# Rounding the normalised features and taking their remainder before the transposition instead of after it, in a four-layer graph network kernel

## What is computed

```python
h = jnp.maximum(_layernorm(x, axis=-1), 0.0); x = x + _L0_gnn_ref(h, adj, ...)   # Chebyshev, K = 4
h = jnp.maximum(_layernorm(x, axis=-1), 0.0); x = x + _L1_gnn_ref(h, adj, ...)   # encoder, 2 attentions, MLP
h = jnp.maximum(_layernorm(x, axis=-1), 0.0); x = x + _L2_gnn_ref(h, adj, ...)   # graph convolution
h = jnp.maximum(_layernorm(x, axis=-1), 0.0); x = x + _L3_gnn_ref(h, adj)        # sum over neighbours
```

## Time and profile before

| | |
|---|---|
| median of 3 runs | 913.66 us |
| the profiled execution: its own time | 909.79 us |
| its span, first to last instruction | 908.0 us |
| TensorE busy | 775.2 us, 85% |
| VectorE busy | 593.0 us, 65% |
| ScalarE busy | 447.5 us, 49% |
| GpSimd busy | 406.3 us, 45% |
| mean granted TensorE clock | 0.973 of full speed |

### The profile page before, as it was taken

One profiled execution on the slowest core, in us unless ns is written; L12 is line 12 of the kernel. 1 busy time (PEld: TensorE's weight loads), 2 busy tenths in 40 slices (PEclk: granted clock), 3 DMA queues, 4 the chain that ended last, 5 costly groups with the idle time before them and its releaser, 6 DMA issues. The chain is left out here.

```text
span 908.0 us, 13130 instructions
## 1 busy us (share of the span) xinstructions
PE 775.2 (85%) x3808; PEld 542.7 (60%) x3808; DVE 593.0 (65%) x1631; ACT 447.5 (49%) x929; POOL 406.3 (45%) x491
## 2 busy tenths in 40 slices
PE   3658798989999798989979898997989899898874
PEld 2435566666667566666756666664666666675543
DVE  3265677686776668677666767766776867765432
ACT  2044646547273644737364463736465472744430
POOL 3144545445553434555443455544454455533301
PEclk9869999999999999999999999999999999999996
DMA  5000101001020200101010010102010010000000
GB/s 170 32 1 1 52 1 40 20 1 59 1 59 0 60 0 6 53 0 58 0 59 0 12 46 0 58 0 59 0 49 9 0 58 0 6 2 6 1 6 6
DMA packets 29264, 22.54 MB, mean 25 GB/s; under 512 B 19488, under 2 KB 21024, under 8 KB 29216
## 3 DMA queue, kind: packets, MB, share of 16 engines
q1 hardware_dynamic: 29216, 22.03, 8.3%
HBM read 19.93 MB, written 2.10 MB: 24 GB/s over the span
## 5 line engine op out<-in xcount | busy, mean ns | idle before, releaser
L605 ACT ACTIVATE negz<-negz,negmax 128x512 f32<-128x512 f32 x128 | 92.3, 721 | 96.8 <-DVE negmax L821 95.7
L425 POOL TENSOR_TENSOR rstd_post<-vareps_post,nhalf 128x4 f32<-128x4 f32 x32 | 39.1, 1221 | 196.2 <-DVE vareps_post L708 196.2
L821 DVE CUSTOM_DVE_ANT_0 negz<-negz,gate 128x512 f32<-128x512 f32 x128 | 102.7, 802 | 23.8 <-DVE negz L815 23.6
L1075 PE MATMUL turn_ps<-pt,v_n 128*128 128x512 f32 x256 | 117.4, 602 | 0.0
L425 POOL TENSOR_TENSOR rstd_pre<-vareps_pre,nhalf 128x4 f32<-128x4 f32 x32 | 34.1, 1067 | 149.5 <-DVE vareps_pre L708 149.5
L955 PE MATMUL pre_ps<-at_hi,u_pair_pre 128*128 128x512 f32 x192 | 87.4, 455 | 7.4 <-DVE u_pair_pre L745 5.2
L815 DVE TENSOR_TENSOR negz<-score_ps,a_nat 128x512 f32<-128x512 f32 x128 | 88.0, 687 | 7.6 <-PE score_ps L1044 5.3
L955 PE MATMUL post_ps<-at_hi,u_pair_post 128*128 128x512 f32 x128 | 55.8, 436 | 38.4 <-DVE u_pair_post L745 38.4
L564 ACT ACTIVATE y_t_pre<-pre_ps 128x512 f32<-128x512 f32 x48 | 28.7, 597 | 118.4 <-PE pre_ps L955 117.6
L1058 PEld LDWEIGHTS turn_ps<-ident,negz 128*128 128x128 f32 x512 | 60.9, 141 | 33.7 <-ACT negz L605 14.6
L955 PE MATMUL pre_ps<-at_lo,u_pair_pre 128*128 128x512 f32 x192 | 78.5, 409 | 0.0
(11 more groups left out here) (138 smaller groups left out, 1838.3 us busy)
## 6 DMA issues: line engine op xcount, KB each, us to landing
a_nat<-in_adj SPq DMA_DIRECT2D x16, 1024.0 KB, 5.7
x_in<-in_x SPq DMA_DIRECT2D x16, 128.0 KB, 2.3
out<-x_out SPq DMA_DIRECT2D x16, 128.0 KB, 1.9
cheb_ws<-in_L_gnn_weight SPq DMA_DIRECT2D x2, 64.0 KB, 5.0
att_w<-in_L_gnn_a_wv SPq DMA_DIRECT2D x2, 64.0 KB, 2.7
att_w<-in_L_gnn_a_wk SPq DMA_DIRECT2D x2, 64.0 KB, 2.5
att_w<-in_L_gnn_a_wq SPq DMA_DIRECT2D x2, 64.0 KB, 2.3
bv_f<-in_L_gnn_a_bv SPq DMA_DIRECT2D x2, 64.0 KB, 2.8
```

The lines of the kernel that those rows point to most:

```text
L425: gp.tensor_tensor(rstd[t][:], vareps[t][:], nhalf[:, 0:RB], ALU.pow)\
L605: sc.activation(probs[:, i, :], negz[:, i, :], ACT.Exp, bias=negmax[:, i:i + 1], scale=-1.0, accum_out=total[:, i:i + 1]).then_inc(probs_d ...
L821: ve.tensor_tensor_reduce(negz[:, i, :], negz[:, i, :], gate[:, i, :], -1.0, 3.0e38, ALU.add, ALU.min, negmax[:, i:i + 1]).then_inc(biased, 1)
L1075: mm = te.matmul(turn_ps[0][:], v_n[a][:, j * P:(j + 1) * P], pt[:, j, :], start=(j == 0), stop=(j == RB - 1))
```

## The change

Both norms now write plain features (`h_nat`, 64 numbers a node) and then a new pair tile `h_pair` of type `float32r`: the rounded features first, and beside them the remainder, a subtraction over 128 x 256 elements. TensorE transposes the pair. ScalarE's copy then yields both parts at once. The step `split_ht` is gone from VectorE, both steps `cheb_ht` and `enc_ht` from its order, and TensorE waits for ScalarE's copy. `set_bias_rows`, which runs once, moves from the first `enc_ht` to the first `norm_enc`.

```diff
@@ vector order
-        split_at2-0 split_at3-0 attend.2-2 mask0.1-1 mask1.1-1 cheb_ht-0 mask2.1-1 
+        split_at2-0 split_at3-0 attend.2-2 mask0.1-1 mask1.1-1 mask2.1-1 
-        mask0.2-1 cheb_fold1-0 stats_enc-0 norm_last-2 mask1.2-1 norm_enc-0 mask2.2-1 enc_ht-0  mask3.2-1  last_fold-2""".split(),
+        mask0.2-1 cheb_fold1-0 stats_enc-0 norm_last-2 mask1.2-1 norm_enc-0 mask2.2-1  mask3.2-1  last_fold-2""".split(),
@@ tiles
-        h_nat = {"pre": sb("h_nat_pre", [P, RB, 2, C]), "post": sb("h_nat_post", [P, RB, C])}
+        h_nat = {t: sb(f"h_nat_{t}", [P, RB, C]) for t in ("pre", "post")}
+        h_pair = sb("h_pair", [P, RB, 2, C], F32R)
@@ def norm_apply(t, chain, g, k):
-                to = h_nat[t][:, :, 0, :] if t == "pre" else h_nat[t][:]
-                one = ve.scalar_tensor_tensor(to, centred[t][:], 0.0, over_blocks(rstd[t][:]),
+                one = ve.scalar_tensor_tensor(h_nat[t][:], centred[t][:], 0.0, over_blocks(rstd[t][:]),
                                               ALU.max, ALU.mult)
@@
                 chain.add(one)
                 dve.wait_ge(chain.sem, chain.so_far())
-                ve.tensor_copy(h_nat[t][:, :, 1, :], to).then_inc(h_ready[t], 1)
+                chain.add(ve.tensor_copy(h_pair[:, :, 0, :], h_nat[t][:]))
+                dve.wait_ge(chain.sem, chain.so_far())
+                ve.tensor_tensor(h_pair[:, :, 1, :], h_nat[t][:], h_pair[:, :, 0, :].bitcast(F32),
+                                 ALU.subtract).then_inc(h_ready[t], 1)
+                if first(g) and k == 1:
+                    set_bias_rows()
@@
-            def split_ht(g, k):
-
-                dve.wait_ge(ht_copied, 2 * g.n + k + 1)
-                ve.tensor_tensor(h_t[C:P, :], pre_ps[C:P, 0, :], h_t[C:P, :].bitcast(F32),
-                                 ALU.subtract).then_inc(ht_split, 1)
-                if first(g) and k == 1:
-                    set_bias_rows()
@@ def turn_h(ready):
                     mm = te.transpose(pre_ps[:, 0, i * P:(i + 1) * P],
-                                      h_nat["pre"][:, i, :, :].rearrange("p a c -> p (a c)"), ident[:])
+                                      h_pair[:, i, :, :].rearrange("p a c -> p (a c)").bitcast(F32),
+                                      ident[:])
@@ cheb_weights and encode on TensorE
-                pe.wait_ge(ht_split, 2 * g.n + 1)
+                pe.wait_ge(ht_copied, 2 * g.n + 1)
-                pe.wait_ge(ht_split, 2 * g.n + 2)
+                pe.wait_ge(ht_copied, 2 * g.n + 2)
```

More of the change, by code:

```diff
@@ L256, in graph_layers @@
         at_split = sem("at_split")
-        ht_split = sem("ht_split")
         u_split = {t: sem(f"u_split_{t}") for t in ("pre", "post")}
@@ L269, in graph_layers @@
         out_done = sem("out_done")
-        dve_pre = Chain(sem("dve_pre"), 2 * 6 + 6)
+        dve_pre = Chain(sem("dve_pre"), 2 * 7 + 6)
         dve_post = Chain(sem("dve_post"), 2 * 5 + 3 + 2)
@@ L466, in cheb_u3 @@
                 pool.wait_ge(dinv_done, g.n + 1)
-                pool_pre.add(gp.tensor_tensor(u3[:], h_nat["pre"][:, :, 0, :],
+                pool_pre.add(gp.tensor_tensor(u3[:], h_nat["pre"][:],
                                               over_blocks(dinv[g.slot][:, 0:RB]), ALU.mult))
@@ L886, in _ @@
                 "split_at1": split_at(1), "split_at2": split_at(2), "split_at3": split_at(3),
-                "cheb_ht": lambda g: split_ht(g, 0),
                 "cheb_weights": cheb_weights, "cheb_fold3": cheb_fold3,
@@ L890, in _ @@
                 "stats_enc": stats_enc, "norm_enc": enc_norm,
-                "enc_ht": lambda g: split_ht(g, 1),
                 **layer(0, mask0=mask(0), mask1=mask(1), mask2=mask(2),
```

## The result

The changed kernel takes 931.17 us (median of 4 runs, 929.95 to 932.27) against 913.39 us before (4 runs, 912.48 to 913.68). The ratio is 1.0196, with a 95% interval from 1.0177 to 1.0215: slower by 17.8 us, where 11.4 us were forecast. The profiled execution has a span of 930.4 us, 22.4 us more than the profiled one of before, at a mean granted clock of 0.956 instead of 0.973.

The account below looks back on a forecast made before the run. TensorE, busy 85% of the span, was taken to bound the kernel; 19.4 − 6.0 − 2.0 − 2.0 + 2.0 = +11.4 us on the 913.7 us median gave 925.1 us, range 915 to 938 us.

Parts of the forecast that it names:

- The holding of the subtraction: norm_cheb on VectorE: new subtraction held behind GpSimd's k_lo, delaying turn_a2 by 1.41 us a round; +19.4 us in all.
- slips in ahead of k_lo: Rival at norm_cheb: subtraction issues before GpSimd's k_lo, delaying turn_a2 only 0.46 us; −3.6 us, 910 us; chance 0.12.
- The two gains: On TensorE, cheb_weights starts 0.24 or 0.69 us sooner a round (−6.0 us), encode 0.13 us sooner (−2.0 us).
- The delay is taken up later in the round: Rival: TensorE waits that don't hang on turn_a2 absorb the delay; −10 us, 904 us; chance 0.05.
- The clock: Behind turn_a2 in the three rounds beginning a loop turn, longer waits lower the clock; +2 us (bounds 0 and +5).
- a rival: Clock falls behind turn_a2 in ordinary rounds too: eight give +12 us, 938 us, all eleven 942 us; chance 0.13.
- The first rounds: Graphs 0 and 1: set_bias_rows begins earlier, graph 1's norm precedes k_lo, two gaps close; −2.0 us (bounds −1 and −2.5).
- nothing behind `split_at` becomes late: ScalarE's copies, the row sum and GpSimd's inverse_roots move as much as TensorE, so cause no further delay; no size added.
- The reference point: Timed runs lie 3.9 us above the profiled execution of before; added to 921.2 us under the profiler, giving 925.1 us.

Follow-up runs that it names:

- e2: Kernel before plus a bn_stats over 128x256 (one SBUF input, result unused) behind the copy in norm_cheb: 920.25 us, ratio 1.0076.
- e4: Changed kernel with norm_cheb moved on VectorE from ahead of split_at0 to behind split_at3: 889.72 us, ratio 0.9747 to the kernel before.
- e3: Kernel before with the change for the encoder's features alone, the Chebyshev features still split behind their transposition: 905.89 us, ratio 0.9931.
- e6: Changed kernel plus seven matmuls with unread results ahead of turn_a2 on TensorE, from graph 2 on: 921.99 us, ratio 1.0107 to the kernel before.
- e8: The changed kernel run again unaltered, on the same chip as e5 and e6: 930.53 us, ratio 1.0190 to the kernel before.
- e5: Kernel before, without the change, with norm_cheb moved behind split_at3 on VectorE: 893.91 us, ratio 0.9771.
- e1: Kernel before plus a subtraction of two SBUF tiles (128x256, result unused) behind the copy in norm_cheb: 951.24 us, ratio 1.0411.

## Why the prediction was right, and where its size was off

**The holding of the subtraction (+1.41 us a round): right.** In the rounds of graphs 3 to 15 the trace after has 1.37 us for it and 1.70 us of wait at `turn_a2`, as written beforehand, and 4.04 us in the rounds that begin a loop turn. (In the round of graph 2, for which 1.1 us were booked, the subtraction was not held in this profile and the wait stayed at 0.20 us.) e2 shows that the holding makes it, and e4 that it costs nothing where nobody waits. The rival "slips in ahead of k_lo" fell: in every round from graph 3 on k_lo took over in the 0.03 us between the rounding's end and the subtraction's issue.

**The two gains (0.24 or 0.69, and 0.13 us a round): right.** TensorE's `encode` marks the rounds. In the round of graph 5, in which the clock stays up in both kernels, first before and then after:

```profile
252.81 0.50 PE L992 MATMUL pre_ps<-h_t,enc_hi 128*128 128x512 f32 x1 [0.36 <-DVE h_t L737]
303.54 0.50 PE L992 MATMUL pre_ps<-h_t,enc_hi 128*128 128x512 f32 x1 [0.36 <-DVE h_t L737]
```
```profile
259.28 0.47 PE L987 MATMUL pre_ps<-h_t,enc_hi 128*128 128x512 f32 x1
311.03 0.48 PE L987 MATMUL pre_ps<-h_t,enc_hi 128*128 128x512 f32 x1
```

That is 50.73 us before and 51.75 us after, +1.02 us, where the terms give 1.41 − 0.24 − 0.13 = +1.04 us. In the round of graph 8, of the other kind, it is 51.19 and 51.78 us, +0.59 us, where they give 1.41 − 0.69 − 0.13 = +0.59 us. "The delay is taken up later in the round" fell with this.

One thing in it was booked in the wrong place: 3.0 us of what was summed at `cheb_weights` are gained by the encoder's half alone (e3).

**The clock (+2 us): a mis-sized term.** In the profiled executions the rounds of graphs 3 to 15 grew by 18.2 us. The waits at `turn_a2` alone make 13 x 1.40 = 18.2 us; `cheb_weights` and `encode` give 5.5 and 1.8 us back; and so 18.2 − 18.2 + 5.5 + 1.8 = 7.3 us are left, which are the clock's: in five rounds `attend.2` to `cheb_ht` took 5.5 to 6.2 us instead of 4.13 us, and in four of the five `turn_a2` was slower too (1.60 to 1.97 us instead of 1.25 us). Before there are two such rounds. I had counted on the three rounds that begin a loop turn alone and given the ordinary ones to a rival. One ordinary round and the last one, with waits of 1.79 and 1.95 us, had it as well; so the rival was right in kind, and its eight or eleven rounds were too many. e6 bounds the term from above: filling takes back 8.5 us, about half of the 16.7 us by which e8 is slower than the kernel before on the same chip, but the two rounds of before are in it. The profile of e8 has the lower clock in the same five rounds as the profile of after.

**The first rounds (−2 us): wrong.** By `encode` of graph 2 the changed kernel was 2.75 us behind, where the terms of graphs 0 to 2 make it some 1.8 us ahead. I had let graph 1's norm move ahead of k_lo. In this profile it didn't:

```profile
63.26 1.38 DVE L724 TENSOR_TENSOR h_pair<-h_nat_pre,h_pair 128x256 fp32r<-128x256 f32 x1
```
```profile
65.38 1.22 PE L911 MATMUL pre_ps<-ident,a_nat 128*128 128x128 f32 x8 [1.58 <-DVE at_lo L733]
```

In the profile of e8, the same kernel, it did: k_lo had to wait for the keys until 62.61, and `turn_a2` waited for nothing.

```profile
62.46 0.42 DVE L724 TENSOR_TENSOR h_pair<-h_nat_pre,h_pair 128x256 fp32r<-128x256 f32 x1
```

TensorE's clock rose later in that execution (0.65 granted from 60 to 66 us, against 1.00 in the profile of after), which may be why the keys were late. And yet e8's `encode` of graph 2 came at 153.01 us, still 1.8 us behind the 151.22 us of before. So the order at k_lo is not what made the term wrong. In graph 0 I had said that nothing behind `split_at` becomes late. It did: with no other work on TensorE, `cheb_prop3` waits for GpSimd's `cheb_u3` (2.20 us before, 2.94 us after), and that hangs on ScalarE's row sums behind the third and fourth part. I had looked at the steady rounds only. Part of this is no effect of the change: the first adjacency matrix landed 0.37 us later in that execution.

**The reference point.** The forecast added the 3.9 us between the profiled execution and the timed median to both kernels. The timed executions of before in the job of e5 to e8 have spans from 909.7 to 913.0 us at clocks from 0.964 to 0.972; the profiled one had 908.0 us at 0.973. So the profiled one was a short execution, and what it lacked may have been drops of the clock, or time in the first rounds. For the second speaks e3: its rounds of graphs 3 to 15 are 6.5 us shorter than those of before in the profiles, just as its median is, but its `encode` of graph 2 came 4.1 us later (155.35 us), and so its profile shows a gain of 2.4 us only. No run separates the two.

**How near the number came by luck.** In the profiles the change costs 22.4 us, 11.0 us more than forecast: about 4.6 us of it up to `encode` of graph 2, 4.9 us in the rounds of graphs 3 to 15 (the clock's), and 1.5 us behind the last `encode`, which I haven't explained. The medians differ by only 17.8 us. The difference comes mostly from the reference: the profiled execution of before was 3.6 us shorter than its median, that of after 1.1 us longer. No term foresaw this, and it brought the number nearer to the forecast.

What stays open: why the clock fell behind a wait of 1.79 us in the round of graph 4 (1.78 us in e8, where it fell as well) and not behind the same wait in the rounds of graphs 7, 10 and 13. The runs show that filling the wait stops it, not which waits bring it about.

## What to carry to other kernels

Before an instruction of VectorE with two SBUF inputs, or a copy between SBUF tiles, is put into an order written by hand, lay GpSimd's timeline beside VectorE's at that place: if GpSimd has work queued there, the price can be the length of GpSimd's instruction instead of its own, and here each of three such instructions in a row paid it. Where a group of such instructions stands ahead of a step that TensorE waits for, move the group behind that step first: here that was worth 20 us without the change (e5) and about 41 us with it (e4), and the change by itself, once it was done, some 3 us. And a wait on TensorE should be priced with the clock behind it: put harmless matmuls into it once, in the kernel before and in the one after. What each gains is the clock's share in it; here only the one after was filled.

## What the runs showed of the hardware that was not expected

- A wait on TensorE of 1.8 us was followed by a stretch at 0.72 of the full clock; waits of 1.9 to 2.1 us (e1) were followed by lower-clock stretches in 8 of 10 ordinary rounds. Filled with 1.67 us of matmuls, the stretches shown were granted 1.00. A kernel with 98 matmuls more ran 8.5 us faster (e6 against e8).
- `bn_stats` over 128 x 256 from one SBUF tile took 0.415 us in the mean right behind a copy, with k_lo or `gate` just issued on GpSimd from graph 1 on, and was not held in any round; the subtraction of two SBUF tiles in the same place took 1.282 us.
- VectorE and GpSimd took turns instruction by instruction at this place: k_lo took over in the 0.03 us between the rounding and the subtraction, which were only a semaphore apart, in every round from graph 3 on of the changed kernel. Without the semaphore between (e1) GpSimd went first in 13 rounds; in two, in which both issued within 0.02 us, the subtraction did and took 0.41 us.
